# Rounding the Gelu values of an MLP on ACT, two feature blocks at a time, instead of on DVE one by one

## Chip, cores and metric

The kernel runs on one core of a Trainium2 chip. The metric is the device time of one execution in microseconds (us), as a median over executions. Engines are named as in the profile: PE (matrix products), ACT (activations and copies), DVE (elementwise arithmetic), POOL, and SP, which issues DMAs.

## What is computed

Two layers of a network over 2 x 1024 tokens of 256 features: conditioning, a state space block, an MLP, pooling, a mixture of experts, attention and a second mixture. The change touches only the MLP of layer 0, whose reference is

```python
res = x
h = _layernorm(x, ln2_w, ln2_b)
h = jax.nn.gelu(h @ mlp_w1.T + mlp_b1, approximate=False) @ mlp_w2.T + mlp_b2
return res + h
```

with `mlp_w1` 1024 x 256 and `mlp_w2` 256 x 1024. Everything is fp32.

## The kernel before

The program is a sequence of phases. Each phase is a block with one hand-written instruction list per engine, ordered by semaphores; all engines meet between phases. The MLP is the second half of `outmlp_phase`.

The 2048 tokens are cut into `NW` = 4 windows of `W` = 512, the 1024 hidden features into `FB` = 8 blocks of 128. The running number of a block is g = 8 w + f. An fp32 product is made of three: each operand is a high part, rounded to fp32r, and a low part, the rest, and `product3` (L1521) issues high x high, high x low and low x high. So each operand needs a rounding (a cast) and a subtraction.

For a window, PE first makes the eight **up products** (6 matmuls of 128x512 each) into a ring of four PSUM banks, `ps[:, g % 4]`. It may start block g when the Gelu of block g - 4 is done (`p_act`, L905). ACT takes each bank with a Gelu into `hid` (named hn in the trace, L970), which waits for `p_up` and, from the second window on, for `p_lo` of the block that last used that part of `hid`. DVE rounds the block into `hidp[0]` (mhid_h, L1023) and subtracts it into `hidp[1]` (mhid_l, L1025), which counts `p_lo`. Then PE makes the **down products** of the window: four token tiles t, each summing over the eight blocks f, 24 matmuls of 128x256. For t = 0 it waits before each f for `p_lo` (L923); for t = 1 to 3 everything is there. DVE adds the results to `X` (L1035) after two adds over the window (L1030, L1031).

There is one `hidp` for all windows, and PE is one queue: the next window's up products follow this window's down products. `split(NW - 1)` on DVE and `affine(NW - 1)` on ACT, which prepare the last window's input (L996, L998 and L945), stand inside window 0, behind its fourth block.

Of the kernel before, what the change touches and what calls it, by code (L numbers as in the profile page):

```python
# [14 lines left out]
ALU = mybir.AluOpType  # L15
# [15 lines left out]
FB = FF // P  # L31
# [388 lines left out]
def chain(k, eng, name):  # L420

    sem, count = k.chains[name]

    def then(ins):
        count[0] += 1
        ins.then_inc(sem, 1)
        eng.wait_ge(sem, count[0])
    return then
# [398 lines left out]
def outmlp_phase(nc, k):  # L827

    ps = k.ps
    with ExitStack() as ctx:  # L830
        def sb(name, shape, dt=F32):
            return ctx.enter_context(nc.sbuf_tensor(name, shape, dt))

        hidp = [sb("mhid_" + part, [P, FB, W], F32R) for part in "hl"]
# [11 lines left out]
        hid = k.hn[:, :, :].rearrange("p i e -> p (i e)").rearrange("p (f t) -> p f t", f=FB)  # L846
# [3 lines left out]
        @block.sync  # L850
        def _(sp):
            sp.dma_start(mw1, k.d["mw1"].rearrange("p j f -> p (j f)")).then_inc(k.s_mw, 16)
            sp.dma_start(mw2, k.d["mw2"].rearrange("p f e -> p (f e)")).then_inc(k.s_mw2, 16)
            sp.dma_start(k.it[:, :], k.d["itok0"].partition_broadcast(P)).then_inc(k.s_it, 16)
            for b in range(B):
                sp.dma_start(k.ih[64 * b:64 * b + 64, :],
                             k.d["itok0"][b:b + 1].partition_broadcast(64)).then_inc(k.s_it, 16)
# [70 lines left out]
        @block.scalar  # L928
        def _(act):
            def normalize(w):  # L930
                act.wait_ge(k.o_var, w + 1)
                nc.scalar.activation(rstd[:, 4 * w:4 * w + 4], mv[:, 4 * w:4 * w + 4, 1], ACT.Sqrt,
                                     bias=k.eps[:, 0:1]).then_inc(k.o_sd, 1)
                act.wait_ge(k.o_sc, w + 1)
                for i in range(4 * w, 4 * w + 4):
                    last = nc.scalar.activation(k.hn[:, i, :], k.res0[:, i, :], ACT.Identity, bias=shift[:, i:i + 1],
                                                scale=rstd[:, i:i + 1])
                last.then_inc(k.o_hn, 1)

            def affine(w):  # L940
                for f in range(EB):
                    act.wait_ge(k.t_2, EB * w + f + 1)
                    if w:
                        act.wait_ge(k.p_in, EB * (w - 1) + f + 1)
                    nc.scalar.activation(turned[:, f, :], ps[:, TURN[f], :], ACT.Identity, bias=k.col("ln2b", f),  # L945
                                         scale=k.col("ln2w", f)).then_inc(k.p_ev, 1)

            for i in range(NT):
                act.wait_ge(k.o_tr, i + 1)
                if i >= 3:  # L950
                    act.wait_ge(k.o_mm, i - 2)
                nc.scalar.copy(ygT[:, i % 3, :, :], ps[:, TR[i % 3], :].rearrange("p (f t) -> p f t", f=4)
                               ).then_inc(k.o_evac, 1)
                if i == 4:
                    act.wait_ge(k.s_mw, 16)
                    nc.scalar.copy(w1[0][:, :], mw1).then_inc(k.p_wh, 1)
                if i == 5:
                    act.wait_ge(k.s_mw2, 16)
                    nc.scalar.copy(w2[0][:, :], mw2).then_inc(k.p_wh, 1)
                if i >= 6 and i % 4 == 2:  # L960
                    normalize(i // 4 - 1)
                if i >= 8 and i % 4 == 0:
                    affine(i // 4 - 2)
            affine(NW - 2)
            normalize(NW - 1)
            for g in range(NW * FB):
                act.wait_ge(k.p_up, g + 1)
                if g >= FB:
                    act.wait_ge(k.p_lo, g - FB + 1)
                nc.scalar.activation(hid[:, g % FB, :], ps[:, g % 4, :], ACT.Gelu,  # L970
                                     bias=k.col("mlpb1", g % FB)).then_inc(k.p_act, 1)
                if g == 3:
                    affine(NW - 1)

# [6 lines left out]
        @block.vector  # L981
        def _(dve):
            then = chain(k, dve, "dve")

            def scale(w):
                at = slice(4 * w, 4 * w + 4)
                dve.wait_ge(k.o_sd, w + 1)
                then(nc.vector.reciprocal(rstd[:, at], rstd[:, at]))
                nc.vector.scalar_tensor_tensor(shift[:, at], mv[:, at, 0], -1.0, rstd[:, at], ALU.mult,
                                               ALU.mult).then_inc(k.o_sc, 1)  # L990

            def split(w):
                for f in range(EB):
                    hi, lo = (p[:, f, w * W:(w + 1) * W] for p in hTp)
                    dve.wait_ge(k.p_ev, EB * w + f + 1)
                    nc.vector.tensor_copy(hi, turned[:, f, :]).then_inc(k.p_inh, 1)  # L996
                    dve.wait_ge(k.p_inh, EB * w + f + 1)
                    nc.vector.tensor_tensor(lo, turned[:, f, :], hi, ALU.subtract).then_inc(k.p_in, 1)  # L998

            then(nc.vector.reciprocal(k.rms[:, :], k.rms[:, :]))  # L1000
            for i in range(NT):
                dve.wait_ge(k.o_mm, i + 1)
                nc.vector.scalar_tensor_tensor(k.res0[:, i, :], ps[:, OUT[i % 3], 0:E], k.rms[:, i:i + 1],
                                               k.res0[:, i, :], ALU.mult, ALU.add).then_inc(k.o_x, 1)
                dve.wait_ge(k.o_x, i + 1)
                last = nc.vector.bn_stats(stats[:, i, :], k.res0[:, i, :])
                if i % 4 == 3:
                    then(last)
                    for n in range(i - 3, i + 1):
                        last = nc.vector.bn_aggr(mv[:, n, :], stats[:, n, :])  # L1010
                    last.then_inc(k.o_var, 1)
                if i % 4 == 0 and i:
                    scale(i // 4 - 1)
                if i % 4 == 3 and i > 4:
                    split(i // 4 - 1)
            scale(NW - 1)
            for w in range(NW):
                if w:
                    dve.wait_ge(k.p_down, 4 * w)
                for f in range(FB):  # L1020
                    g = w * FB + f
                    dve.wait_ge(k.p_act, g + 1)
                    nc.vector.tensor_copy(hidp[0][:, f, :], hid[:, f, :]).then_inc(k.p_hi, 1)  # L1023
                    dve.wait_ge(k.p_hi, g + 1)
                    nc.vector.tensor_tensor(hidp[1][:, f, :], hid[:, f, :], hidp[0][:, f, :],  # L1025
                                            ALU.subtract).then_inc(k.p_lo, 1)
                    if g == 3:
                        split(NW - 1)
                xs, r = k.X[:, 4 * w:4 * w + 4, 0:E], k.res0[:, 4 * w:4 * w + 4, :]
                then(nc.vector.tensor_tensor(xs, xs, r, ALU.add))  # L1030
                then(nc.vector.tensor_tensor(xs, xs, k.row("mlpb2", 0, E).unsqueeze(1).to_broadcast([P, 4, E]), ALU.add))  # L1031
                for t in range(4):
                    i = 4 * w + t
                    dve.wait_ge(k.p_down, i + 1)
                    nc.vector.tensor_tensor(k.X[:, i, 0:E], k.X[:, i, 0:E], ps[:, DOWN + t, 0:E],  # L1035
                                            ALU.add).then_inc(k.p_x, 1)
# [1674 lines left out]
```

## Time and profile before

| | before |
|---|---|
| median of 3 runs | 1599.75 us (1597.16 to 1599.82) |
| profiled execution | 1592.62 us, of which the span is 1590.8 us |
| PE busy in the span | 1371.9 us (86%) |
| DVE busy | 999.9 us (63%) |
| ACT busy | 637.3 us (40%) |
| mean granted PE clock | 0.929 of full speed |
| the MLP's four windows | about 374 to 464 us of the span |

Times in the trace are counted from the start of the span. Busy time of PE is modelled from pipelined matmuls, so the pace of PE is better read from start to start of its instructions. "Idle before" is the time an engine sat before an instruction, and the name behind the arrow is what ended it.

### The profile page before, as it was taken

To read this page: it belongs to the slowest core of one execution; us is meant where nothing else is said; L and a number is where in the kernel's file an instruction comes from. 1 tells how busy PE (TensorE), PEld (TensorE's weight loads), DVE (VectorE), ACT (ScalarE), POOL (GpSimd) and SP (SyncE) were. 2 spreads that over 40 slices of the span, in tenths; PEclk is the share of its full clock that TensorE was granted. 3 is DMA by queue.
4 is the path that set the end of the run, shared out by engine and by line. 5 is a ranking of instruction groups with operands and counts; after the bars stand their busy time and mean duration, and the time that the engine had idled before them with its cause. 6 is when DMAs were issued, how large, how long until landed. Compare 5 with 4: busy or idle time off the path is not lost. (4 is left out here: it accounts for less than half of the span.)

```text
span 1590.8 us, 24738 instructions
## 1 busy us (share of the span) xinstructions
PE 1371.9 (86%) x8658; PEld 1137.0 (71%) x8659; DVE 999.9 (63%) x1799; ACT 637.3 (40%) x1315; POOL 489.6 (31%) x469
## 2 busy tenths in 40 slices
PE   8848699988998699999999999798998996819992
PEld 3435366577975489999989999457886885519992
DVE  4864889946658774664565545767787774135652
ACT  3424876553222334323323343125565561215540
POOL 1330199620000170660260402422212100045663
PEclk9977899989998699999999999999999998759996
DMA  6000000010000131120020000000000000263423
GB/s 225 0 0 1 13 1 1 0 54 1 1 1 1 53 112 47 53 85 20 0 106 0 0 0 0 27 1 1 1 1 1 1 1 0 80 244 128 176 79 114
DMA packets 25242, 64.88 MB, mean 41 GB/s; under 512 B 4354, under 2 KB 16532, under 8 KB 20242
## 3 DMA queue, kind: packets, MB, share of 16 engines
q1 hardware_dynamic: 23634, 59.85, 10.5%
q0 software_dynamic: 1536, 4.10, 0.8%
q8 instruction: 42, 0.69, 0.2%
q14 instruction: 30, 0.25, 0.0%
HBM read 54.07 MB, written 9.44 MB: 40 GB/s over the span
## 5 line engine op out<-in xcount | busy, mean ns | idle before, releaser
L1676 ACT ACTIVATE hT<-ps,eb 128x256 f32<-128x256 f32 x296 | 124.3, 472 | 272.2 <-PE ps L1521 272.2
L1696 DVE TENSOR_TENSOR ehidl<-hT,ehidh 128x512 fp32r<-128x512 f32 x148 | 132.7, 897 | 5.1
L1998 ACT ACTIVATE pr<-ps,nmax 128x256 f32<-128x256 f32 (+7 forms) x128 | 94.0, 738 | 102.9 <-DVE nmax L2028 102.7
L1694 DVE CAST ehidh<-hT 128x512 fp32r<-128x512 f32 x148 | 89.6, 605 | 72.6 <-ACT hT L1676 72.6
L1521 PE MATMUL ps<-kh,qz 128*128 128x512 f32 (+3 forms) x384 | 124.3, 378 | 3.4 <-ACT pr L1998 1.9
L1703 DVE SCALAR_TENSOR_TENSOR X<-ps,wE,X 128x256 f32 x74 | 35.9, 485 | 106.7 <-PE ps L1521 96.9
L1521 PE MATMUL ps<-ew_1h,ehidh 128*128 128x256 f32 x304 | 85.8, 282 | 8.6 <-DVE ehidl L1696 8.3
L2028 DVE TENSOR_REDUCE nmax<-ps 128x1 f32<-128x256 f32 (+7 forms) x128 | 91.0, 749 | 1.0 <-PE ps L1938 0.6
L1600 POOL TENSOR_TENSOR eb<-eb1s,consts 128x8 f32<-128x8 f32 x8 | 1.8, 227 | 288.7 <-PE ps L1521 282.5
L1521 PE MATMUL ps<-ew_0h,ehidh 128*128 128x256 f32 x288 | 81.4, 283 | 7.9 <-DVE ehidl L1696 7.5
L1521 PE MATMUL ps<-hTh,ew_0h 128*128 x288 | 82.4, 286 | 5.1 <-issue 5.1
L1521 PE MATMUL ps<-hTh,ew_1h 128*128 x304 | 85.5, 281 | 0.0
L1521 PEld LDWEIGHTS ps<-kh,qz 128*128 128x128 f32 x384 | 75.7, 198 | 13.4 <-ACT pr L1998 4.8
L1521 PE MATMUL ps<-hTh,ew_1l 128*128 x304 | 85.0, 279 | 0.0
L1521 PE MATMUL ps<-hTl,ew_1h 128*128 x304 | 84.9, 279 | 0.0
L1521 PE MATMUL ps<-ew_1l,ehidh 128*128 128x256 f32 x304 | 84.3, 277 | 0.0
L1521 PE MATMUL ps<-ew_1h,ehidl 128*128 128x256 f32 x304 | 84.2, 277 | 0.0
L1521 PE MATMUL ps<-hTh,ew_0l 128*128 x288 | 81.4, 283 | 0.0
L1867 POOL CAST qz<-qh 32x256 fp32r<-32x256 f32 x64 | 27.9, 436 | 173.8 <-PE ps L1938 154.2
L1521 PE MATMUL ps<-hTl,ew_0h 128*128 x288 | 81.4, 283 | 0.0
L1958 PE MATMUL ps<-v,hT 128*128 128x64 f32 x576 | 76.8, 279 | 5.2 <-ACT hT L1989 5.0
L1521 PE MATMUL ps<-ew_0l,ehidh 128*128 128x256 f32 x288 | 79.9, 278 | 0.0
(523 smaller groups left out, 4252.0 us busy)
## 6 DMA issues: line engine op xcount, KB each, us to landing
ew1s<-in_ew_dram SPq DMA_DIRECT2D x9, 1024.0 KB, 4.7
ew2s<-in_ew_dram SPq DMA_DIRECT2D x9, 1024.0 KB, 6.9
fw1s<-in_fw_dram SPq DMA_DIRECT2D x8, 1024.0 KB
fw2s<-in_fw_dram SPq DMA_DIRECT2D x8, 1024.0 KB
slot_rows<-zero SPq DMA_DIRECT2D x1, 2560.0 KB, 10.6
xr<-slot_rows SPq DMA_DIRECT2D x5, 512.0 KB, 6.0
xT<-in_xT_dram SPq DMA_DIRECT2D x4, 512.0 KB, 7.5
X<-in_x_dram SPq DMA_DIRECT2D x1, 2048.0 KB, 18.5
```

The lines of the kernel that those rows point to most:

```text
L1521: last = nc.tensor.matmul(out, lhs[a], rhs[b], start=(start and n == 0), stop=(stop and n == 2), **kw)
L1600: nc.gpsimd.tensor_tensor(b1[q][:, :], b1s[q][:, :], k.const("ones", 0, FB), ALU.mult)
L1676: nc.scalar.activation(hid[:, f, :], ps[:, f // 2, (f % 2) * JOB:(f % 2 + 1) * JOB], ACT.Gelu, bias=b1[q][:, f:f + 1]).then_inc(k.e_act, 1)
L1694: nc.vector.tensor_copy(hi[:, f, :], hid[:, f, :]).then_inc(k.e_dhi, 1)
L1696: nc.vector.tensor_tensor(lo[:, f, :], hid[:, f, :], hi[:, f, :], ALU.subtract).then_inc(k.e_lo, 1)
L1703: nc.vector.scalar_tensor_tensor(x, ps[:, DOWN + t, 0:E], wE2[:, bass.ds(e * NT + blk * TILES + t, 1)], x, ALU.mult, ALU.add).then_inc(k.e ...
L1867: last = nc.gpsimd.tensor_copy(k.qz[r, i % QZ, n, :, s, :], part[r, :, i * P:(i + 1) * P])
L1958: last = nc.tensor.matmul(ps[:, PV + i % 2, h * 64:(h + 1) * 64], dT[:, n % 2, j, :], k.v[:, i - c + j, h * 64:(h + 1) * 64], start=(h == ...
L1998: nc.scalar.activation(pr[:, n % 3, u, 0:wide], half(n, u, wide), ACT.Exp, bias=nmax[:, n % 2, u:u + 1], accum_out=sums[:, u, n:n + 1]).th ...
L2028: nc.vector.tensor_reduce(nmax[:, n % 2, u:u + 1], half(n, u, wide), AX.X, ALU.max, negate=True).then_inc(k.a_max, 1)
```

## The change

ACT makes the high parts. After each odd block (the second of a pair) it waits for its own Gelu, and from window 1 on for the down products of the window before, and copies two blocks at once, 128x1024, from `hid` into `hidp[0]`. DVE no longer casts; it subtracts two blocks at once and counts `p_lo` by two. `split(NW - 1)` now stands behind the second pair, again behind four blocks.

```diff
@@ scalar @@
                 nc.scalar.activation(hid[:, g % FB, :], ps[:, g % 4, :], ACT.Gelu,
                                      bias=k.col("mlpb1", g % FB)).then_inc(k.p_act, 1)
+                if g % 2:
+                    f = slice(g % FB - 1, g % FB + 1)
+                    if g >= FB:
+                        act.wait_ge(k.p_down, 4 * (g // FB))
+                    act.wait_ge(k.p_act, g + 1)
+                    nc.scalar.copy(hidp[0][:, f, :], hid[:, f, :]).then_inc(k.p_hi, 1)
                 if g == 3:
                     affine(NW - 1)
@@ vector @@
-                for f in range(FB):
-                    g = w * FB + f
-                    dve.wait_ge(k.p_act, g + 1)
-                    nc.vector.tensor_copy(hidp[0][:, f, :], hid[:, f, :]).then_inc(k.p_hi, 1)
+                for q in range(FB // 2):
+                    g, f = w * FB // 2 + q, slice(2 * q, 2 * q + 2)
                     dve.wait_ge(k.p_hi, g + 1)
                     nc.vector.tensor_tensor(hidp[1][:, f, :], hid[:, f, :], hidp[0][:, f, :],
-                                            ALU.subtract).then_inc(k.p_lo, 1)
-                    if g == 3:
+                                            ALU.subtract).then_inc(k.p_lo, 2)
+                    if g == 1:
                         split(NW - 1)
```

On ACT, the start of window 0 (the semaphores that a row waits for are in brackets, x4 means four such rows; L945 is `affine`):

```order
 L970 ACT_TABLE_LOAD
-L970 ACTIVATE hn<-ps,cols 128x512 [waits p_up] x4
+L970 ACTIVATE hn<-ps,cols 128x512 [waits p_up] x2
+L977 CAST mhid_h<-hn 128x1024 [waits p_act]
+L970 ACTIVATE hn<-ps,cols 128x512 [waits p_up] x2
+L977 CAST mhid_h<-hn 128x1024 [waits p_act]
 L945 ACTIVATE hturn<-ps,cols 128x512 [waits p_in,t_2] x2
```

A copy of 1024 elements has come behind every second Gelu, and each waits for the Gelu ahead of it; no table load has come in.

On DVE, windows 1 to 3 begin so in the kernel before (seven more pairs of cast and subtract like these follow, then L1030):

```order
L1023 CAST mhid_h<-hn 128x512 [waits p_act,p_down]
L1025 TENSOR_TENSOR mhid_l<-hn,mhid_h 128x512 [waits p_hi]
L1023 CAST mhid_h<-hn 128x512 [waits p_act]
L1025 TENSOR_TENSOR mhid_l<-hn,mhid_h 128x512 [waits p_hi]
L1023 CAST mhid_h<-hn 128x512 [waits p_act]
```

and so in the changed kernel:

```order
L1029 TENSOR_TENSOR mhid_l<-hn,mhid_h 128x1024 [waits p_hi,p_down]
L1029 TENSOR_TENSOR mhid_l<-hn,mhid_h 128x1024 [waits p_hi] x3
L1034 TENSOR_TENSOR X<-X,res 128x4x256
L1035 TENSOR_TENSOR X<-X,rows 128x4x256 [waits own_dve]
L1039 TENSOR_TENSOR X<-X,ps 128x256 [waits p_down,own_dve]
```

Sixteen short rows of a window have become four long ones, and what DVE waits for in each is no longer the Gelu but ACT's copy.

## Rows read from the trace of the kernel before

**Rows 1.** The page, part 1: busy time, share, instructions.

```profile
PE 1371.9 (86%) x8658; PEld 1137.0 (71%) x8659; DVE 999.9 (63%) x1799; ACT 637.3 (40%) x1315; POOL 489.6 (31%) x469
```

**Rows 2.** Busy time by stretch: the MLP, and the stretch behind it.

```profile
core 0: us, PE busy (x) PEld busy (x) DVE busy (x) ACT busy (x) POOL busy (x), PEclk, DMA share, GB/s
...
374.00:464.00 90.00, 86.15 (x560) 78.60 (x560) 53.48 (x92) 24.24 (x35) 0.00 (x0) 1.00 0.00 1
464.00:555.00 91.00, 72.76 (x330) 43.94 (x330) 69.01 (x195) 27.41 (x52) 11.15 (x10) 0.82 0.06 24
```

**Rows 3.** Waits from 370 to 470 us: total, times, longest.

```profile
ACT hn L970 <- PE ps L1521: 54.3, 27, 14.1
...
DVE mhid_h L1023 <- ACT hn L970: 13.1, 22, 4.1
...
PE ps L1521 <- DVE mhid_l L1025: 1.1, 3, 0.4
```

**Rows 4.** Timeline, window 1's end: start, duration, engine, instruction; last two Gelu.

```profile
405.55 0.69 ACT L970 ACTIVATE hn<-ps,cols 128x512 f32<-128x512 f32 x1 [0.67 <-PE ps L1521]
406.91 0.69 ACT L970 ACTIVATE hn<-ps,cols 128x512 f32<-128x512 f32 x1 [0.68 <-PE ps L1521]
```

**Rows 5.** Timeline, the same place on PE: 1st, 2nd and 19th down matmul.

```profile
406.71 0.29 PE L1521 MATMUL ps<-mw_h,mhid_h 128*128 128x256 f32 x1
406.84 0.28 PE L1521 MATMUL ps<-mw_l,mhid_h 128*128 128x256 f32 x1
...
408.88 0.28 PE L1521 MATMUL ps<-mw_h,mhid_h 128*128 128x256 f32 x1
```

**Rows 6.** Timeline, the same place on DVE: the last block's parts, first add.

```profile
407.63 0.43 DVE L1023 CAST mhid_h<-hn 128x512 fp32r<-128x512 f32 x1 [0.21 <-ACT hn L970]
408.10 0.69 DVE L1025 TENSOR_TENSOR mhid_l<-hn,mhid_h 128x512 fp32r<-128x512 f32 x1
408.70 1.22 DVE L1030 TENSOR_TENSOR X<-X,res 128x1024 f32<-128x1024 f32 x1
```

**Rows 7.** Timeline, window 0 on DVE: the split, sixth and eighth subtraction.

```profile
380.28 0.42 DVE L996 CAST mhT_h<-hturn 128x512 fp32r<-128x512 f32 x1
...
382.41 0.42 DVE L1023 CAST mhid_h<-hn 128x512 fp32r<-128x512 f32 x1
...
383.93 0.69 DVE L1025 TENSOR_TENSOR mhid_l<-hn,mhid_h 128x512 fp32r<-128x512 f32 x1
...
386.05 0.69 DVE L1025 TENSOR_TENSOR mhid_l<-hn,mhid_h 128x512 fp32r<-128x512 f32 x1
```

**Rows 8.** Timeline, PE in window 0.

```profile
376.03 1.09 PE L884 MATMUL ps<-consts,hn 128*128 128x128 f32 x8 [2.48 <-ACT hn L970]
...
382.45 0.29 PE L1521 MATMUL ps<-mw_h,mhid_h 128*128 128x256 f32 x1
...
384.67 0.39 PE L1521 MATMUL ps<-mw_h,mhid_h 128*128 128x256 f32 x1 [0.26 <-DVE mhid_l L1025]
384.89 0.29 PE L1521 MATMUL ps<-mw_l,mhid_h 128*128 128x256 f32 x1
...
386.80 0.39 PE L1521 MATMUL ps<-mw_h,mhid_h 128*128 128x256 f32 x1 [0.43 <-DVE mhid_l L1025]
```

**Rows 9.** Instructions from 374 to 464 us by form: busy, mean ns, idle.

```profile
L1025 DVE TENSOR_TENSOR mhid_l<-hn,mhid_h 128x512 fp32r<-128x512 f32 x32 | 22.2, 693 | 1.1
...
L970 ACT ACTIVATE hn<-ps,cols 128x512 f32<-128x512 f32 x32 | 21.8, 690 | 54.3 <-PE ps L1521 54.3
L1023 DVE CAST mhid_h<-hn 128x512 fp32r<-128x512 f32 x32 | 13.6, 426 | 13.5 <-ACT hn L970 13.1
```

**Rows 10.** Instructions of the whole span by form, ACT's and DVE's.

```profile
L1178 ACT CAST hTh<-hT 128x512 fp32r<-128x512 f32 x6 | 3.7, 619 | 20.5 <-DVE hT L1279 20.5
...
L1393 ACT CAST ew_0h<-ew1s 128x2048 fp32r<-128x2048 f32 x1 | 1.9, 1898 | 3.8 <-DMA eb1s<-in_eb_dram 3.8
...
L1247 DVE TENSOR_TENSOR both_m<-pm,sm 128x1024 f32<-128x1024 f32 x1 | 1.2, 1221 | 0.0
...
L1696 DVE TENSOR_TENSOR ehidl<-hT,ehidh 128x512 fp32r<-128x512 f32 x148 | 132.7, 897 | 5.1
```

**Rows 11.** Timeline, window 0 on ACT.

```profile
375.29 2.42 ACT L970 ACTIVATE hn<-ps,cols 128x512 f32<-128x512 f32 x4
377.59 1.47 ACT L945 ACTIVATE hturn<-ps,cols 128x512 f32<-128x512 f32 x2
```

**Rows 12.** Waits from 555 to 1000 us, the experts.

```profile
PE ps L1521 <- DVE ehidl L1696: 15.8, 19, 1.4
```

## The prediction

> **What bounds the kernel now.** I read the shares of the page first: PE is busy 86% of the span, far ahead of DVE and ACT [rows 1]. Then the stretch of the MLP by itself: in 90 us PE is busy 86.15, DVE 53.48, ACT 24.24, POOL not at all, at a granted clock of 1.00 [rows 2]. The list of waits says the same from the other side: ACT waits 54.3 us for PE, DVE's casts wait 13.1 us for ACT, and PE waits only 1.1 us, three times, for a subtraction [rows 3]. So PE sets the pace, and the question for the change is when the high and low parts are ready compared with the matmul that reads them. Work that DVE gets rid of is worth nothing unless PE was waiting for it.
>
> Windows 1 to 3 are alike, so I take the end of window 1. The Gelu come every 1.36 us (405.55, 406.91), which is the pace of PE's up products, and each has 0.67 or 0.68 us of idle time ahead of it [rows 4]. PE starts the down products at 406.71 and a matmul every 0.12 us, so a block f of three takes 0.36 us; the 19th matmul, the first of block 6, starts at 408.88 and block 7 would be wanted at 408.88 + 0.36 = 409.24 [rows 5]. The last Gelu ends at 407.60 [rows 4], DVE casts at 407.63 and subtracts from 408.10 to 408.79 [rows 6]. Block 7 is ready 0.45 us before PE wants it. That is the whole slack.
>
> Window 0 is another case. PE has made up products ahead, so ACT and DVE are behind it: DVE works without a gap, its sixth and eighth subtractions end at 383.93 + 0.69 = 384.62 and 386.05 + 0.69 = 386.74 [rows 7], and PE starts on those blocks at 384.67 and 386.80 [rows 8]. Here DVE is what PE waits for.
>
> **The change, part by part.** *Removed*: 32 casts of 426 ns, 13.6 us of DVE [rows 9]. *Replaced*: 32 subtractions of 693 ns (22.2 us) [rows 9] by 16 of 1024 elements. No fp32r subtraction of 1024 is in the trace; the f32 one of the same size takes 1.221 us [rows 10], and L1030 takes 1.22 in this very window [rows 6]. I take 1.22, so 19.5 us. The bounds: in the experts the same 128x512 subtraction takes 897 ns instead of 693 [rows 9, 10], a factor 1.29, which would make it 1.58; POOL works there and is idle here [rows 2], so I keep 1.22. *Added on ACT*: 16 copies of 128x1024. ACT casts 512 elements in 619 ns and 2048 in 1898 ns [rows 10]; on the line between them 1024 take 619 + 512 x (1898 - 619)/1536 = 1.05 us, 16.7 us in all. The bounds are the two rows themselves, 0.62 and 1.90. *Added waits*: the wait for ACT's own Gelu. From one engine to the next, and on DVE from cast to subtract, the next starts about 0.03 us after the end [rows 4, 6]; I take 0.03. The wait for the down products of the previous window costs nothing: PE makes them before the up products whose Gelu ACT has just done.
>
> *Does ACT keep up?* A pair costs 0.69 + 0.69 + 0.03 + 1.05 = 2.46 us, against 2 x 1.36 = 2.72 us of PE [rows 4]. The first Gelu of a pair may start 0.3 us late because the copy is still running, but the second is on time, and PE's ring has four banks, about 4.1 us. So the up products do not wait: cost nothing, the cover being that ring. Were a copy 1.90 us, a pair would take 3.31 us and ACT would be some 0.6 us later with each pair.
>
> *Windows 1 to 3, the end of a window.* The last Gelu ends at 407.60 as before. Copy of blocks 6 and 7: 407.63 to 408.68. Subtraction of both: 408.71 to 409.93. PE can start on block 6 0.05 us after that, as it did in window 0 (384.62 to 384.67) [rows 7, 8], at 409.98. It would have wanted it at 408.88 [rows 5]. The wait is 1.10 us. A matmul that starts after such a wait takes 0.22 us until the next instead of 0.12 (384.67, 384.89) [rows 5, 8]: 0.10 more. So **1.20 us a window, 3.6 us in three**. Two things add up: a path of copy and subtraction of 2.3 us in the place of 1.16, and that block 6 now waits for block 7.
>
> *Earlier pairs.* Blocks 4 and 5: their Gelu end near 404.88, copy to 405.96, subtraction to 407.21; PE wants them at 406.71 + 4 x 0.36 = 408.15. No wait. *The adds of X* start 1.1 us later on DVE, but the bank of t = 0 is wanted again only in the next window. Behind t = 3, the last add of the phase follows PE as before.
>
> *Window 0.* Starts of back-to-back Gelu are 0.58 apart ((2.42 - 0.69)/3) [rows 11]. Copy of blocks 0 and 1: 376.6 to 377.6; Gelu 2 and 3 to 378.8; copy to 379.9; the two affines (1.47) [rows 11] to 381.2, where before they were done at 379.06; Gelu 4 and 5 to 382.4; copy to 383.45; Gelu 6 and 7 to 384.6; copy to 385.7. DVE subtracts 0 and 1, 2 and 3 (to 381.1), then the split, 2.13 us long (380.28 to 382.41) [rows 7], to 383.2, then 4 and 5 from 383.5 to 384.7, and 6 and 7 from 385.7 to 386.9. PE, at the down products from 382.45 [rows 8], waits for block 4 until 384.75 and for block 6 until 387.0. The tile t = 0 ends at 387.0 + 0.10 + 0.72 = 387.8; before, at 386.80 + 0.22 + 0.24 = 387.26 [rows 8]. **0.55 us more.** DVE has less to do here, but ACT, which now carries the copies, the affines and the Gelu in one queue, is late in its place.
>
> Sum: 3.6 + 0.55 = 4.15 us. All of it stands on PE, which works through to the end of the phase, and the engines meet there, so I see nothing that absorbs it. The profiled execution took 1592.62 us, its span 1590.8; with the change 1596.8. The median of the runs shown is 7.1 us above that execution; the same 4.15 on 1599.75 gives 1603.9. What a measurement here can tell from no change is about 0.2%, 3.2 us, so the expected loss lies just above it.
>
> **Rivals.**
> *A, window 0 gains.* DVE is what PE waits for in window 0. A cast and a subtraction of a block take 1.06 us there (half of 384.62 to 386.74), eight of them 8.5, and four long subtractions 4.9: 3.6 us less. If ACT got there in time, t = 0 would run through, from 382.45 in 8 x 0.36 us to 385.33 instead of 387.26: 1.93 us gained, the sum 3.6 - 1.93 = +1.7, 1601.4 us. Against it: by the rows ACT's queue has the last copy done at 385.7 only. It decides when that copy ends before about 383.4. The Trainium skill ("VectorE: DVE Perf Modes", Rules for kernel authors) says to minimize the number of DVE operations; by that alone the change is good, and this is the time it would give. The trace shows DVE as the late engine in one window of four only.
> *B, the copies are shorter*: at 0.62 us, the lower bound, a window loses 1.20 - 0.43 = 0.77, three lose 2.3; in window 0 four copies end 4 x 0.43 = 1.7 earlier, the last at 384.0, and t = 0 ends at 386.1, 1.1 gained. +1.2, 1601.0 us. For it: no row has this size. Against it: a copy of twice the elements would have to cost no more than one of 512.
> *C, the clock behind the MLP: the one that ends faster.* From 464 to 555 us PE is busy 72.76 us at a granted clock of 0.82 [rows 2], in work with pauses. The change shifts when that work starts by 4 us. If less of it fell at 1.2 GHz, at most 72.76 x 0.18 = 13.1 us could come back; a third of it, 4.4, cancels the loss, and for faster by 0.2% it must be 7.4, more than half: 1596.5. Nothing in the trace says that it is drawn to that side; it may as well cost 3 us (1607).
> *D, the new pauses cost clock.* PE now stops for 1.1 us in each window. After a pause of 2.48 us at 376.03 [rows 8] the stretch still has a granted clock of 1.00 [rows 2], and the experts have 19 such waits of up to 1.4 us [rows 12]. If the next tile's 24 matmuls ran at 1.2 GHz after all, 24 x 0.12 = 2.9 us more in each of three windows: +12.8, 1612.5 us. The Trainium skill ("TensorE: Matmul & The Clock Gate", Part 1) says that idleness puts the array back to half rate, which speaks against every change that adds pauses; by the pauses of this trace, these are too short for it.
> *E, the subtraction takes 1.58 us* as if POOL shared with it: +0.36 in four windows, 5.6 in all, 1605.3 us.
>
> **How the numbers follow.** My forecast, with its bounds 1603 to 1605.5: 0.58. A 0.08, B 0.12, C 0.10 (0.03 of it faster, the rest to either side), D 0.03, E 0.09. The likeliest is +4.15, so 1604.0. Medians of three runs of such a kernel move by 1 to 2 us (before: 1597.16 to 1599.82). The range goes from 1600.5, which takes in A and B with a low median, to 1607.5, which takes in E with a high one; D and the faster end of C are left out. Slower by over 0.2% needs over 1602.95: my case and E less what scatter takes under that line, 0.67. Within 0.2%: A, B and that scatter, 0.28. Faster: 0.05.
>
> **What would show it.** The changed trace should have 16 casts on ACT of 1.05 us and 16 subtractions of 1.22; in windows 1 to 3 one idle of PE of 1.1 us each, ended by the subtraction of blocks 6 and 7, and each window 1.2 us longer; in window 0 two waits of PE, before blocks 4 and 6; ACT's wait for PE down from 54.3 to some 41 us (less the 16.7 of the copies, plus the pauses of PE); a clock of 1.00. Wrong it would be if PE waited in the up products for `p_act` (the copy too long), if window 0 got shorter (A), or if the difference lay outside 374 to 470 us (C).

## The result, and the profile after

| | before | after |
|---|---|---|
| median of 20 runs each, same chips | 1598.47 us | 1601.05 us |
| profiled execution, its span | 1592.62, 1590.8 us | 1601.78, 1600.0 us |
| ratio of the times, 95% interval | | 1.0027 (1.0018 to 1.0037) |
| mean granted PE clock | 0.929 | 0.927 |

The change makes the kernel slower by 0.27% (0.18 to 0.37%), 4.3 us of 1598.5; the medians alone differ by 2.6. First the page's busy times, the counterpart of [rows 1], and the two stretches, of [rows 2]:

```profile
PE 1379.9 (86%) x8658; PEld 1144.1 (72%) x8659; DVE 984.5 (62%) x1751; ACT 652.5 (41%) x1331; POOL 489.9 (31%) x469
```

```profile
374.00:464.00 90.00, 84.36 (x544) 76.61 (x545) 37.45 (x43) 38.11 (x50) 0.00 (x0) 1.00 0.00 1
464.00:555.00 91.00, 75.26 (x337) 46.66 (x336) 67.12 (x195) 23.75 (x46) 11.11 (x10) 0.79 0.06 24
```

In the stretch of the MLP DVE has 16.0 us less to do and ACT 13.9 more, and in the same 90 us PE makes 16 matmuls fewer. (The stretch is cut at fixed times: the changed MLP runs from 372.32 to 467.53 us.) The clock is still 1.00. Where the time went is in the waits from 370 to 470 us (of [rows 3]):

```profile
ACT hn L970 <- PE ps L1525: 41.9, 15, 12.4
DVE mhid_l L1029 <- ACT mhid_h L977: 34.4, 16, 5.9
...
PE ps L1525 <- DVE mhid_l L1029: 5.3, 5, 1.3
```

PE's wait for the low parts has grown from 1.1 us in three pieces to 5.3 us in five, +4.2. The new instructions by form (of [rows 9]: busy, mean ns, idle):

```profile
L1029 DVE TENSOR_TENSOR mhid_l<-hn,mhid_h 128x1024 fp32r<-128x1024 f32 x16 | 19.6, 1225 | 34.4 <-ACT mhid_h L977 34.4
L977 ACT CAST mhid_h<-hn 128x1024 fp32r<-128x1024 f32 x16 | 16.8, 1050 | 1.2
```

The end of window 1, the place of [rows 4 to 6], on ACT, DVE and PE:

```profile
405.89 0.69 ACT L970 ACTIVATE hn<-ps,cols 128x512 f32<-128x512 f32 x1 [0.32 <-PE ps L1525]
406.66 1.05 ACT L977 CAST mhid_h<-hn 128x1024 fp32r<-128x1024 f32 x1
```

```profile
405.09 1.23 DVE L1029 TENSOR_TENSOR mhid_l<-hn,mhid_h 128x1024 fp32r<-128x1024 f32 x1 [1.50 <-ACT mhid_h L977]
407.81 1.22 DVE L1029 TENSOR_TENSOR mhid_l<-hn,mhid_h 128x1024 fp32r<-128x1024 f32 x1 [1.50 <-ACT mhid_h L977]
```

```profile
407.73 0.29 PE L1525 MATMUL ps<-mw_h,mhid_l 128*128 128x256 f32 x1
409.09 0.39 PE L1525 MATMUL ps<-mw_h,mhid_h 128*128 128x256 f32 x1 [1.08 <-DVE mhid_l L1029]
409.31 0.29 PE L1525 MATMUL ps<-mw_l,mhid_h 128*128 128x256 f32 x1
```

Read it as a chain: the last Gelu ends at 405.89 + 0.69 = 406.58, the copy runs 406.66 to 407.71, the subtraction 407.81 to 409.03, PE goes on at 409.09. The matmul before was at 407.73, and the next was due 0.12 later, at 407.85. PE loses 1.24 us in the pause (the row says 1.08, since the ends of matmuls are modelled) and 0.10 more as the first matmul takes 0.22 to the next.

Window 0, the place of [rows 7, 8, 11], on ACT, DVE and PE:

```profile
377.16 1.05 ACT L977 CAST mhid_h<-hn 128x1024 fp32r<-128x1024 f32 x1
378.11 1.44 ACT L945 ACTIVATE hturn<-ps,cols 128x512 f32<-128x512 f32 x2
379.45 1.26 ACT L970 ACTIVATE hn<-ps,cols 128x512 f32<-128x512 f32 x2
380.74 1.05 ACT L977 CAST mhid_h<-hn 128x1024 fp32r<-128x1024 f32 x1
381.69 1.26 ACT L970 ACTIVATE hn<-ps,cols 128x512 f32<-128x512 f32 x2
382.98 1.05 ACT L977 CAST mhid_h<-hn 128x1024 fp32r<-128x1024 f32 x1
```

```profile
381.89 1.23 DVE L1029 TENSOR_TENSOR mhid_l<-hn,mhid_h 128x1024 fp32r<-128x1024 f32 x1 [0.23 <-ACT mhid_h L977]
384.14 1.23 DVE L1029 TENSOR_TENSOR mhid_l<-hn,mhid_h 128x1024 fp32r<-128x1024 f32 x1 [1.02 <-ACT mhid_h L977]
```

```profile
383.17 0.39 PE L1525 MATMUL ps<-mw_h,mhid_h 128*128 128x256 f32 x1 [0.79 <-DVE mhid_l L1029]
...
385.42 0.38 PE L1525 MATMUL ps<-mw_h,mhid_h 128*128 128x256 f32 x1 [1.27 <-DVE mhid_l L1029]
```

ACT has no gap beyond 0.03 us here, and DVE now waits for it before both of the last subtractions; before, DVE had no gap.

The length of each window is read from the timeline: window 0 from the Gelu's table load to the first Gelu of window 1, the others from first Gelu to first Gelu, the last to the first copy behind the MLP (L453). The marks are 374.00, 397.39, 419.83, 442.28 and 464.75 before, and 372.32, 396.36, 420.05, 443.83 and 467.53 after. Window 1's two marks, before and after:

```profile
397.39 0.69 ACT L970 ACTIVATE hn<-ps,cols 128x512 f32<-128x512 f32 x1 [14.05 <-PE ps L1521]
419.83 0.69 ACT L970 ACTIVATE hn<-ps,cols 128x512 f32<-128x512 f32 x1 [12.23 <-PE ps L1521]
```

```profile
396.36 0.69 ACT L970 ACTIVATE hn<-ps,cols 128x512 f32<-128x512 f32 x1 [12.33 <-PE ps L1525]
420.05 0.69 ACT L970 ACTIVATE hn<-ps,cols 128x512 f32<-128x512 f32 x1 [12.34 <-PE ps L1525]
```

Every experiment below is read in this way as well.

| us | window 0 | 1 | 2 | 3 | sum |
|---|---|---|---|---|---|
| before | 23.39 | 22.44 | 22.45 | 22.47 | 90.75 |
| after | 24.04 | 23.69 | 23.78 | 23.70 | 95.21 |
| difference | 0.65 | 1.25 | 1.33 | 1.23 | 4.46 |

The two profiled spans differ by more, 9.2 us. Outside the MLP the stages of these two profiles, whose code is the same, differ too: the one that contains the experts is 4.3 us longer after, the others 1.6 shorter to 1.3 longer.

### The profile page after: what moved, and what is told of

It is laid out like the page before. It is cut to its first block and busy times, and to the rows that moved or that the text cites. A ratio compares the mean times of both kernels' runs of the same rounds, so it can differ in the third digit from the quotient of the medians.

```text
span 1600.0 us, 24731 instructions
## 1 busy us (share of the span) xinstructions
PE 1379.9 (86%) x8658; PEld 1144.1 (72%) x8659; DVE 984.5 (62%) x1751; ACT 652.5 (41%) x1331; POOL 489.9 (31%) x469
```

## The experiments

Every experimental kernel carries one small edit that has nothing to do with the MLP: a loop of the experts takes its first job number through a clamp at zero. The first experiment is this edit alone on the kernel before. Where the expectations name theories by a letter, L says that the parts of a window's last pair come late, Q that ACT's load is what costs; A to E are the prediction's rivals.

**The clamp alone.**

```diff
+            base_reg = [eng.alloc_register(f"base_{eng.engine.name}_{q}") for q in range(2)]
...
-                    base = eng.snap(rows[q][1], min_val=0, max_val=E0 * NB)
+                    eng.reg_alu(base_reg[q], rows[q][1], 0, ALU.max)
+                    base = eng.snap(base_reg[q], min_val=0, max_val=E0 * NB)
```

> The kernel before, and one register operation more per expert slot and engine (the first job number of an expert is clamped at zero or above), which every kernel of the study below carries. It shows what that operation costs and what this way of timing can tell. [...] In the MLP: PE waits 1.1 us in all for subtractions, all in window 0, as before.

Measured: 1.0003 (0.9991 to 1.0014); windows 23.37, 22.44, 22.46, 22.47. It costs nothing that can be told, in the windows nothing at all. The interval shows what such a ratio can tell: about 2 us to either side, more than one window loses.

**The last pair of each window back on DVE, block by block.** ACT rounds pairs 0 to 2, DVE casts and subtracts blocks 6 and 7 singly.

```diff
@@ scalar @@
-                if g % 2:
+                if g % 2 and g % FB < FB - 2:
@@ vector @@
-                for q in range(FB // 2):
+                for q in range(FB // 2 - 1):
...
+                for f in range(FB - 2, FB):
+                    dve.wait_ge(k.p_act, w * FB + f + 1)
+                    nc.vector.tensor_copy(hidp[0][:, f, :], hid[:, f, :]).then_inc(k.p_hi, 1)
...
+                                            ALU.subtract).then_inc(k.p_lo, 1)
```

> The change, but blocks 6 and 7 of each window are cast and subtracted on DVE one by one, as before; ACT still makes the high parts of blocks 0 to 5 in pairs (12 copies instead of 16). Theory L (the last pair is late for PE): in windows 1 to 3 block 6 is ready 0.7 us and block 7 about 0.4 us before PE wants it, no wait there, 3.6 us come back; in window 0 ACT's queue still delays blocks 4 and 6 and tile t = 0 ends within 0.2 us of where it did before. Sum +0.1 us against the kernel before, ratio 1.000. Rival Q (what costs is ACT's fuller queue, wherever the copies stand): three quarters of the loss stay, +3.2 us, 1.002, with PE waiting in windows 1 to 3. Rival C (the loss lies in the clock of the stretch behind the MLP): the MLP's length says nothing about the total.

Measured: 1.0016 (1.0005 to 1.0028); windows 23.67, 22.75, 22.73, 22.75, sum 91.90. Of the 1.23 to 1.33 us a window, 0.94 to 1.05 are gone. That was the question: the loss of windows 1 to 3 lies in the last pair, since the other three pairs are still made as in the changed kernel. But 0.3 a window stay that I had not expected. DVE and PE at the end of window 1:

```profile
405.08 1.23 DVE L1029 TENSOR_TENSOR mhid_l<-hn,mhid_h 128x1024 fp32r<-128x1024 f32 x1 [1.49 <-ACT mhid_h L977]
406.23 0.42 DVE L1035 CAST mhid_h<-hn 128x512 fp32r<-128x512 f32 x1
...
407.75 0.69 DVE L1037 TENSOR_TENSOR mhid_l<-hn,mhid_h 128x512 fp32r<-128x512 f32 x1
```

```profile
408.08 0.29 PE L1531 MATMUL ps<-mw_h,mhid_l 128*128 128x256 f32 x1
408.49 0.39 PE L1531 MATMUL ps<-mw_h,mhid_h 128*128 128x256 f32 x1
408.71 0.28 PE L1531 MATMUL ps<-mw_l,mhid_h 128*128 128x256 f32 x1
```

The long subtraction of blocks 4 and 5 keeps DVE until 406.2, so the four short operations behind it run without a gap and end at 407.75 + 0.69 = 408.44; block 7 was wanted at 408.08 + 0.12 = 408.20. The pause is 0.29 and the restart 0.10. Pairing one place earlier delays the next by itself.

**All blocks rounded by ACT, but singly.** ACT copies 128x512 after each Gelu, DVE subtracts block by block.

```diff
@@ scalar @@
-                if g % 2:
-                    f = slice(g % FB - 1, g % FB + 1)
-                    if g >= FB:
-                        act.wait_ge(k.p_down, 4 * (g // FB))
-                    act.wait_ge(k.p_act, g + 1)
+                f = g % FB
+                if g >= FB:
+                    act.wait_ge(k.p_down, 4 * (g // FB))
+                act.wait_ge(k.p_act, g + 1)
...
@@ vector @@
-                for q in range(FB // 2):
-                    g, f = w * FB // 2 + q, slice(2 * q, 2 * q + 2)
+                for f in range(FB):
+                    g = w * FB + f
...
-                                            ALU.subtract).then_inc(k.p_lo, 2)
-                    if g == 1:
+                                            ALU.subtract).then_inc(k.p_lo, 1)
+                    if g == 3:
                         split(NW - 1)
```

> The change without its pairs: ACT copies each block by itself (32 copies of 128x512, 0.62 us) and DVE subtracts each by itself (0.69 us). ACT is busier than in the change: 32 x 0.62 = 19.8 us of copies instead of 16.8. Theory L: the last block is ready 0.69 + 0.09 + 0.62 + 0.03 + 0.69 + 0.05 = 2.2 us after its Gelu starts, that is 2.4 us after the first down matmul, and PE wants it after 2.5: no wait in windows 1 to 3. A Gelu and its copy take about 1.30 us against PE's pace of 1.36. In window 0 ACT is the late engine, its last copy ends near 387.1 on the old clock of the trace, and tile t = 0 ends 1.0 us later than before. Sum +1.0 us, 1.0006. Rival Q: more work on ACT than in the change, so at least the change's loss, +4.3 us or more, 1.003.

Measured: 1.0010 (0.9998 to 1.0022); windows 24.03, 22.45, 22.45, 22.47, sum 91.40. ACT at the end of window 1:

```profile
404.16 0.69 ACT L970 ACTIVATE hn<-ps,cols 128x512 f32<-128x512 f32 x1
...
405.53 0.69 ACT L970 ACTIVATE hn<-ps,cols 128x512 f32<-128x512 f32 x1
406.31 0.62 ACT L976 CAST mhid_h<-hn 128x512 fp32r<-128x512 f32 x1
```

ACT has more to do than in the changed kernel (32 copies of 0.62 are 19.8 us against 16.8) and still keeps PE's pace of 1.36; windows 1 to 3 are as before to 0.01 us. So ACT's load is not what costs there. Window 0, where PE is ahead and ACT's queue is the limit, loses 0.64, much as with the change (0.65); 1.0 was expected.

**Pairs, but all on DVE.** The kernel before with casts and subtractions of 128x1024, nothing on ACT.

```diff
@@ vector, kernel before @@
-                for f in range(FB):
-                    g = w * FB + f
-                    dve.wait_ge(k.p_act, g + 1)
+                for q in range(FB // 2):
+                    g, f = w * FB // 2 + q, slice(2 * q, 2 * q + 2)
+                    dve.wait_ge(k.p_act, 2 * g + 2)
...
-                                            ALU.subtract).then_inc(k.p_lo, 1)
-                    if g == 3:
+                                            ALU.subtract).then_inc(k.p_lo, 2)
+                    if g == 1:
                         split(NW - 1)
```

> The pairs alone: DVE casts and subtracts two blocks at once, ACT does only the Gelu. A cast of 1024 on DVE lies on the line between 0.43 us (512) and 1.23 (2048): 0.69. Theory L: in windows 1 to 3 the subtraction of blocks 6 and 7 ends 0.89 + 0.03 + 0.69 + 0.03 + 1.23 = 2.87 us after the first down matmul, PE wants block 6 after 2.16: a wait of 0.75 and 0.10 for the restart, 0.85 a window, 2.6 in three. In window 0 the pairs save DVE little, tile t = 0 ends 0.1 us earlier. Sum +2.4 us, 1.0015. Rival Q: no work is added to ACT, so nothing is lost, 1.000.

Measured: 1.0018 (1.0005 to 1.0030); windows 23.56, 23.27, 23.38, 23.30, sum 93.51. DVE and PE at the end of window 1:

```profile
405.60 0.69 DVE L1023 CAST mhid_h<-hn 128x1024 fp32r<-128x1024 f32 x1 [0.70 <-ACT hn L970]
406.40 1.23 DVE L1025 TENSOR_TENSOR mhid_l<-hn,mhid_h 128x1024 fp32r<-128x1024 f32 x1
```

```profile
406.73 0.29 PE L1521 MATMUL ps<-mw_h,mhid_l 128*128 128x256 f32 x1
407.68 0.39 PE L1521 MATMUL ps<-mw_h,mhid_h 128*128 128x256 f32 x1 [0.67 <-DVE mhid_l L1025]
```

Pairing alone costs 2.76 us of the change's 4.46, 0.83 to 0.93 in each of windows 1 to 3. The move to ACT adds 0.40 to 0.42 in each of these: 1.05 - 0.69 = 0.36 us for the longer copy, and 0.05 because ACT's copy starts 0.08 behind ACT's own Gelu where DVE's cast starts 0.03 behind it (404.88 + 0.69 = 405.57, 405.60). In window 0 it adds 0.48.

**Four blocks at once.** The changed kernel with copies and subtractions of 128x2048, to make the same mechanism large.

```diff
-                if g % 2:
-                    f = slice(g % FB - 1, g % FB + 1)
+                if g % 4 == 3:
+                    f = slice(g % FB - 3, g % FB + 1)
...
-                for q in range(FB // 2):
-                    g, f = w * FB // 2 + q, slice(2 * q, 2 * q + 2)
+                for q in range(FB // 4):
+                    g, f = w * FB // 4 + q, slice(4 * q, 4 * q + 4)
...
-                                            ALU.subtract).then_inc(k.p_lo, 2)
-                    if g == 1:
+                                            ALU.subtract).then_inc(k.p_lo, 4)
+                    if g == 0:
                         split(NW - 1)
```

> The change doubled: ACT copies four blocks at once (8 copies of 128x2048, about 1.90 us) and DVE subtracts four at once (2.29 us). Theory L (PE waits for the last group, by the length of copy and subtraction and by how early its first block is wanted): group 4 to 7 is ready 0.89 + 0.09 + 1.90 + 0.03 + 2.29 + 0.05 = 5.2 us after the first down matmul, block 4 is wanted after 1.44, so PE waits 3.8 us and 0.1 for the restart: 3.9 in each of windows 1 to 3. In window 0 tile t = 0 ends 1.9 us later. The MLP, from the table load to the first copy of the next phase, grows from 90.7 to about 104.3 us, ratio 1.0085. Rival D (pauses of PE cost clock): pauses of 3.8 us bring the granted clock of the MLP clearly under 1.00 and add a few us more. Rival N (fewer operations are what counts): DVE has 8 subtractions in the place of 64 operations, no loss.

Measured: 1.0111 (1.0096 to 1.0126); windows 26.90, 27.81, 27.65, 29.03, sum 111.39, 20.6 us above before where some 13.5 were expected. By the ratio the whole kernel is 17.7 us slower (15.3 to 20.1), a little less than its windows; why is not shown. PE in window 1, from the last matmul ahead of the pause on:

```profile
411.07 0.28 PE L1525 MATMUL ps<-mw_h,mhid_l 128*128 128x256 f32 x1
415.00 0.48 PE L1525 MATMUL ps<-mw_h,mhid_h 128*128 128x256 f32 x1 [3.65 <-DVE mhid_l L1029]
415.27 0.42 PE L1525 MATMUL ps<-mw_l,mhid_h 128*128 128x256 f32 x1
415.49 0.41 PE L1525 MATMUL ps<-mw_h,mhid_l 128*128 128x256 f32 x1
...
418.26 0.41 PE L1525 MATMUL ps<-mw_h,mhid_h 128*128 128x256 f32 x1
...
418.63 0.28 PE L1525 MATMUL ps<-mw_h,mhid_l 128*128 128x256 f32 x1
418.75 0.28 PE L1525 MATMUL ps<-mw_h,mhid_h 128*128 128x256 f32 x1
```

The pause came out as worked out: the next matmul was due at 411.07 + 0.12 = 411.19 and started 3.81 us later, where 3.8 was expected (the row says 3.65). But behind it a matmul starts every 0.213 us (415.27 to 418.26, 14 steps) and only from 418.63 on every 0.12; the list by stretch gives a granted clock of 0.83 from 414 to 424 us and 0.94 over 374 to 464. That is the lower of the two levels, 1.2 GHz, for 3.5 us. Behind the last window's pause matmuls come at that pace for 6 us (470.83 to 476.59), and this window is the longest. From the matmul behind the pause to the last of the window, the four windows take 1.5, 1.5, 1.3 and 2.7 us more than at 0.12 a matmul, which is most of what the expectation lacked. Rival D of the prediction is real, then, but for pauses of 3.8 us; behind the 1.2 us of the changed kernel the third matmul already comes 0.13 us after the second (409.31, 409.44).

**The split behind the last block, in the kernel before.** To see what window 0 of the kernel before is made of: `split(NW - 1)` is not wanted by PE until the last window.

```diff
-                    if g == 3:
+                    if g == 7:
                         split(NW - 1)
```

> The kernel before, with one edit: split(3), the preparation of the last window's input on DVE (2.13 us), stands behind the eighth block of window 0 instead of behind the fourth. Theory L says that in window 0 DVE is what PE waits for, so t = 0 runs through without a wait and ends 1.9 us earlier; windows 1 to 3 as before. MLP 90.7 to 88.8 us, ratio 0.9988. A rival that holds DVE unimportant everywhere expects no difference.

Measured: 1.0001 (0.9988 to 1.0013); windows 21.57, 22.45, 22.45, 22.47. Window 0 is 1.82 us shorter: DVE was what PE waited for there, as the prediction had it. In the time of the whole kernel these 1.8 us cannot be told.

**The same in the changed kernel.** It is rival A's own test: if DVE is what is late in window 0 after the change, it must gain there.

```diff
-                    if g == 1:
+                    if g == 3:
                         split(NW - 1)
```

> The change, with split(3) behind the fourth pair of window 0 instead of the second: the edit that shortened window 0 by 1.8 us in the kernel before. By the theory that ACT's queue, not DVE, is the late one in window 0 of the changed kernel, it gives nothing: the copies of blocks 4 and 5 and of 6 and 7 end where they did, window 0 stays at 24.0 us from the table load to the first Gelu of window 1, windows 1 to 3 at 23.7 each, MLP 95.2 us. Rival A (window 0 hangs on DVE's work): window 0 falls to about 22.2, MLP 93.4.

Measured: windows 24.04, 23.78, 23.69, 23.80. Window 0 has not moved by 0.01 us. DVE there:

```profile
381.97 1.23 DVE L1029 TENSOR_TENSOR mhid_l<-hn,mhid_h 128x1024 fp32r<-128x1024 f32 x1 [2.36 <-ACT mhid_h L977]
```

The 2.1 us of the split have become idle time, 0.23 before and 2.36 now; ACT's copy is what it waits for. The ratio, however, was 1.0050 (1.0037 to 1.0063), against 1.0027 for the change. I therefore ran both once more, beside the same runs of the kernel before.

> The change itself, with the register operation per expert slot that the study's kernels carry. The MLP takes 95.2 us from the table load to the first copy of the next phase, as in the changed kernel, and the ratio lies near 1.0028 if what counts is the MLP's 4.5 us alone. It is timed beside change_split_late, whose MLP is as long (95.3) and whose ratio was 1.0050: if the difference belongs to that edit, the two differ again by about 0.002; if it is chance in where the granted clock falls in the attention phase, long after the MLP, they need not.

> The same kernel as change_split_late, beside change_guarded on one chip. Its MLP is again 95.3 us. If the 3.3 us that its attention phase took more than in most profiles (347.2 us against 344) come with the kernel, they are there again and the ratio is again 1.005; if not, the ratio falls towards 1.003.

Measured: the changed kernel 1.0040 (1.0026 to 1.0054), with the split late 1.0034 (1.0024 to 1.0043); window sums 95.23 and 95.10. The difference did not come back. The two profiles of the kernel with the split late have spans of 1603.0 and 1596.3 us. Of these 6.7 us, 3.6 lie in the experts (469.8 against 466.2 us, from the first expert's weights to the attention's) and 2.9 in the attention phase (347.2 against 344.3, from its weights to the second mixture's). The attention phase, first profile and repeat of the same kernel (columns as in [rows 2]):

```profile
1018.00:1365.00 347.00, 310.44 (x1856) 247.85 (x1856) 253.02 (x483) 154.13 (x380) 70.22 (x136) 0.97 0.01 4
```

```profile
1014.00:1358.00 344.00, 310.27 (x1856) 248.62 (x1854) 252.28 (x483) 154.01 (x380) 69.98 (x136) 0.96 0.01 4
```

The same 1856 matmuls took 347.2 us once and 344.3 once, so the edit does not decide which. In steps of 10 us the granted clock is below 1.00 in seven of 34 steps in both (in the 7th, 8th, 11th, 23rd, 24th, 32nd and 33rd, and in the 7th, 8th, 9th, 20th, 31st, 32nd and 33rd). The longer profile has the higher mean clock, so the clock does not explain its length. Over all profiles of the study this phase has lengths from 343.9 to 347.4 us, and the longest of them belongs to the fastest kernel (the last one below). A profile is one execution: what made the ratio 1.0050 in the first runs stays open, and the intervals of the two sets of runs of this kernel just overlap.

**The transposes first.** On top of the late split in the kernel before: PE makes `normalized(NW - 1)` ahead of its wait for the first Gelu, so ACT's affines get their input sooner.

```diff
+                    if g == 4:
+                        normalized(NW - 1)
                     if g >= 4:
                         pe.wait_ge(k.p_act, g - 3)
                     if g == 3:
                         pe.wait_ge(k.o_x, NT)
-                    if g == 4:
-                        normalized(NW - 1)
```

> split_late, and PE makes the transposes of the last window's input before it waits for the first Gelu, while ACT loads its table. The up products of block 4 start 0.85 us earlier; DVE, now 0.4 us behind at block 7, takes back about 0.5. MLP 88.5 us, 2.2 less than before, ratio 0.9986.

Measured: 0.9992 (0.9983 to 1.0002); windows 21.25, 22.44, 22.46, 22.47, sum 2.13 below before.

**The Gelu's table loaded early.** On top of that, ACT takes a Gelu of one element ahead of its wait for the layer norm's last factors, so that the table load falls into that wait.

```diff
+                if w == NW - 1:
+                    nc.scalar.activation(early[:, :], k.eps[:, 0:1], ACT.Gelu)
                 act.wait_ge(k.o_sc, w + 1)
...
         turned = sb("hturn", [P, EB, W])
+        early = sb("early", [P, 1])
```

> transposes_first, and a Gelu of one element behind the last Sqrt, so that the table load (1.28 us) falls into ACT's wait for DVE ahead of the last normalization. The first Gelu starts 1.3 us earlier. From the start of that normalization (L936, 371.90 us in the kernel before) to the first copy of the next phase it took 92.85 us before; here 89.2, 3.6 less, ratio 0.9977. If the four Identity activations needed another table, a second load would stand between and 2.6 us of it would come back.

Measured: 0.9978 (0.9966 to 0.9991). From the last layer norm (the group that begins at 370.96 here) to the first copy behind the MLP 89.73 us, against 92.85 before; 3.12 less, where some 3.6 less was expected. ACT, and PE in window 1:

```profile
368.89 1.28 ACT L936 ACT_TABLE_LOAD   x1
370.18 0.20 ACT L936 ACTIVATE early<-eps 128x1 f32<-128x1 f32 x1
370.96 2.08 ACT L939 ACTIVATE hn<-res,shift,rstd 128x256 f32<-128x256 f32 x4 [0.57 <-DVE shift L992]
```

```profile
396.21 0.39 PE L1524 MATMUL ps<-mhT_h,mw_h 128*128 128x512 f32 x1
396.44 0.40 PE L1524 MATMUL ps<-mhT_l,mw_h 128*128 128x512 f32 x1
```

The table load is hidden (the Gelu follow the layer norm at 372.94), but the up matmuls start every 0.233 us instead of every 0.227, and the windows 1 to 3 are 22.59, 22.59, 22.60, 0.14 longer. The 48 up matmuls of window 1 take 0.27 us more than before; its down matmuls gain 0.13, for they start every 0.1187 us instead of every 0.1200 (402.62 to 413.78, 94 steps). The new tile of 4 bytes a partition was allocated ahead of `mhT_h` and `mhT_l`; that it moved them, and by 4 bytes, is argued from the order, for their addresses are in no trace. So:

**The same, with the small tile behind them.**

```diff
-        early = sb("early", [P, 1])
...
         hTp = [sb("mhT_" + part, [P, EB, N], F32R) for part in "hl"]
+        early = sb("early", [P, 1])
```

> table_early, with the one-element tile of the early Gelu allocated behind the parts of the MLP's input instead of ahead of them. In table_early the up products, whose moving operand these parts are, came every 0.233 us instead of 0.227, and a window took 22.59 us instead of 22.45; the down products kept their pace. If the 4 bytes by which the tile shifted the parts are the cause, the pace returns to 0.227, a window to 22.45, and the stretch from the last normalization to the first copy of the next phase falls from 89.73 to about 89.1 us, ratio near 0.9975. If it is something else (the early Gelu itself, the clock), the windows stay at 22.6.

Measured: 1592.49 us, 0.9966 (0.9953 to 0.9979); 89.29 us from the layer norm to the copy, windows 22.44 and 22.45. PE in window 1:

```profile
396.06 0.39 PE L1524 MATMUL ps<-mhT_h,mw_h 128*128 128x512 f32 x1
396.28 0.39 PE L1524 MATMUL ps<-mhT_l,mw_h 128*128 128x512 f32 x1
```

This version is faster than both kernels: 0.34% faster than the one before, and its interval lies wholly below that of the change (1.0018 to 1.0037). The up matmuls are back at 0.227 us and the down matmuls at 0.1200, so both paces went with the place of the tile. This kernel leaves the Gelu's parts as they were and takes 3.56 us out of the stretch from the layer norm to the end of the MLP, all of it around window 0, the one window in which PE waited for others. The ratio says 5.4 us (3.4 to 7.5).

## Why the prediction was right

The forecast was 1604.0 us, +4.15; measured 1601.05, and +4.3 by the ratio. The absolute time is 3.0 us lower: 1.3 of it because this batch of runs of the kernel before lies lower (1598.47 against 1599.75), the rest because the two medians differ by 2.6 us only. It lies below the 1603 to 1605.5 of the prediction's own case and at the times that it gave for A (1601.4) and B (1601.0), so the total alone would have pointed to a wrong rival; only the windows tell them apart.

*PE sets the pace, and the block after the last Gelu is what counts*: right. The last pair alone taken back returned about 1 us of the 1.27 of a window, and more work on ACT, in single blocks, cost windows 1 to 3 nothing.

*Windows 1 to 3, +1.20 each*: measured 1.25, 1.33, 1.23. The durations were right (copies 1.050 us from the line through two rows, forecast 1.05; subtractions 1.225, forecast 1.22). Too small were the crossings: 0.08 from the Gelu to ACT's own copy and 0.10 from the copy to DVE, where 0.03 each was taken. The rows behind the 0.03 were of 512 elements, and of this size it holds: behind ACT's single copy of 512 DVE starts 0.04 after its end (406.31 + 0.62 = 406.93, 406.96). Behind DVE's own cast of 1024 it is 0.11 (405.60 + 0.69 = 406.29, 406.40). The crossings make the pause with its restart 1.34 instead of 1.20; in windows 1 and 3 about 0.1 of it comes back behind the restart (below).

*Pairs cost by themselves*: the prediction named two parts, the longer path and that block 6 now waits for block 7. Pairs on DVE show that pairing costs 0.83 to 0.93 us a window, but they hold both parts, since their path is longer too (405.60 to 407.63, 2.03 us in the place of 1.16). The rows part them: block 6 is wanted 0.36 us before block 7, so of the pause of 1.24 us 0.36 comes from waiting for both, and the rest, 0.88, from a path that is longer by more than the slack. No run made one part without the other.

*Window 0, +0.55*: measured 0.65, with the two pauses before blocks 4 and 6 as forecast. Rival A (DVE late, window 0 gains 1.7) fell: with the split out of DVE's way window 0 is the same, as ACT's one queue is late. The Trainium skill ("VectorE: DVE Perf Modes", Rules for kernel authors) says, for chained DVE operations, to minimize their number. As a rule for the time of this kernel it would lead astray: 48 operations fewer on DVE [rows 1] went with 4.46 us more in the MLP, and pairs on DVE alone, 32 fewer, with 2.76 more.

*B and E*: both fell by the measured durations, 1.050 and 1.225. *C*: the stretch behind the MLP, 464 to 555 us, is not a like stretch of the two programs once everything is shifted; from the first copy to the first expert's weights it took 80.6 us against 79.3, so nothing came back. Nor are these 1.3 us a finding: over all profiles of the study this stretch took 78.1 to 80.9 us. *D*: fell for the pauses of the changed kernel, 1.1 us by the row (clock 1.00 in the whole MLP), and was found in the kernel with 3.65 us. The Trainium skill ("TensorE: Matmul & The Clock Gate", Part 1) says that idleness puts the array back to half rate. The kernel with four blocks at once agrees with it. The prediction read it as speaking against every added pause, and that reading fails: the changed kernel kept a clock of 1.00.

*Window 0's schedule*: the last copy was forecast to end at 385.7; it ends at 382.98 + 1.05 = 384.03 in a trace whose table load is 1.68 us earlier, that is at 385.71.

*The sum*: 4.15 forecast, 4.46 in the windows. That the ratio gives 4.3 as well is partly luck, since its interval is 2.9 to 5.9 us and the same change measured once more with the clamp gave 6.4 (1.0040). ACT's wait for PE is 41.9 us, forecast some 41.

## What to carry to other kernels

An engine with idle time on average can still be the one that is late at the handover, so ask not how much work a merged instruction saves but when its first and last results are ready against the matmul that wants them; a pair makes its first block wait for the second. Where a consumer catches up with its producer at the end of a window, keep the last blocks small and on the shortest path, and look for time in the window in which the bound engine really waits (here window 0: 3.6 us by moving a split, eight transposes and a table load). An edit of 2 us in 1600 is read in its own stretch of the trace, since the rest of the program wanders by more than that.

## What was not expected of the hardware

A pause of 3.65 us of PE by the row cost another 1.6 us behind it (17 matmuls from 415.00 to 418.63, at 0.12 they take 2.04; the restart's 0.15 is in it): they start every 0.213 us. Behind a like pause in the last window the low clock lasted 6 us and cost 2.7, so even equal pauses do not cost the same. On the other side pauses of 1.1 us and one of 2.48 us [rows 8] cost no clock. Where the step lies between them was not tried.

A tile of 4 bytes a partition, allocated ahead of the moving operand, made the 128x512 fp32r matmuls that read it start every 0.233 us instead of 0.227, 2.6% more; with the tile behind that operand the 0.227 was back. Which address matters, and why, was not tried.

Behind the pause of 1.1 us the matmuls start every 0.1186 us (409.56 to 418.34, 74 steps) where the kernel before has 0.1200 (408.88 to 418.12, 77 steps), which gives back 0.1 us. It is not the pause alone that decides: behind window 2's pause the changed kernel keeps 0.1200, which is why that window lost 1.33 us and its neighbours 1.25 and 1.23, and the kernel with the small tile ahead has 0.1187 without a pause. The cause is open.

Phases took several us more or less from profile to profile: the experts 466.2 to 471.2 us in the kernels with the clamp and 464.8 and 469.1 in the two without it, the attention 343.9 to 347.4 with the same code in all. The dips of the granted clock come at other places, but in the attention the longer of two profiles had the higher mean clock. What makes a phase long or short stays open.
